# Turning attention probabilities with VectorE block transposes and DMAs instead of TensorE, and repeating the feed-forward q and k by DMA

## What is computed

```python
xn = layernorm(x)
# branch 1: 16 heads of 64, causal
q, k, v = split(xn @ W_qkv);  q, k = rotary(q), rotary(k)
weights = softmax(where(mask, q @ k.T / 8, -1e9))
y = (weights @ v) @ W_out
# branch 2: 16 heads of 8, not causal, then a layer of 8 experts, top 2
q, k, v = xn @ Wq + bq, xn @ Wk + bk, xn @ Wv + bv
ctx = softmax(q @ k.T / sqrt(8)) @ v
x2 = xn + layernorm(ctx @ Wo + bo) * g1 + be1
moe = top2 experts of x2, weighted by the gate's softmax
out = x + y + x2 + layernorm(moe) * g2 + be2
```

## Time and profile before

| what | value |
|---|---|
| median of 3 runs (lowest, highest) | 1271.35 us (1267.77, 1273.54) |
| span of the profiled execution | 1270.3 us |
| TensorE busy in it | 1159.3 us (91%) |
| VectorE busy | 928.0 us (73%) |
| ScalarE busy | 892.0 us (70%) |
| GpSimd busy | 811.5 us (64%) |
| mean granted TensorE clock | 0.978 |

### The profile page before, as it was taken

One profiled execution on the slowest core, in us unless ns is written; L12 is line 12 of the kernel. 1 busy time (PEld: TensorE's weight loads), 2 busy tenths in 40 slices (PEclk: granted clock), 3 DMA queues, 4 the chain that ended last, 5 costly groups with the idle time before them and its releaser, 6 DMA issues.

```text
span 1270.3 us, 25325 instructions
## 1 busy us (share of the span) xinstructions
PE 1159.3 (91%) x9387; PEld 741.3 (58%) x9387; DVE 928.0 (73%) x2336; ACT 892.0 (70%) x1841; POOL 811.5 (64%) x730
## 2 busy tenths in 40 slices
PE   4779999999999999999999999999999999899986
PEld 3355565655666565655656556665656556575655
DVE  7666487885878857896687848787687866778546
ACT  3567867487766868578775887668776796748860
POOL 3655774577855767568864778467675587645760
PEclk8799999999999999999999999999999999999998
DMA  4000100011000110001100011001000011000000
GB/s 144 34 34 18 43 35 17 26 39 38 34 18 26 51 43 26 18 26 59 39 13 35 26 43 42 18 26 51 34 29 24 25 35 51 18 17 34 34 18 9
DMA packets 34110, 42.87 MB, mean 34 GB/s; under 512 B 5694, under 2 KB 17216, under 8 KB 33988
## 3 DMA queue, kind: packets, MB, share of 16 engines
q1 hardware_dynamic: 30516, 38.31, 8.2%
q10 hardware_dynamic: 3472, 2.95, 0.8%
HBM read 5.60 MB, written 2.10 MB: 6 GB/s over the span
## 4 chain that ended last, share of the span: by engine, by line
PE 59%; DVE 17%; ACT 14%; issue 4%; POOL 4%; DMA 1%; SPq 0%; ACTq 0%; DVEq 0%; POOLq 0%
PE work L1319 7%; PE work L1233 7%; PE work L1334 6%; PE work L1346 6%; PE work L1235 6%; PE work L1234 6%; PE work L1396 5%; DVE fnmax L1071 5%; ACT fpt L884 5%; PE work L1362 4%; ACT pn L926 4%; DVE work L1193 3%; PE work L1371 3%; PE work L1386 3%; ACT pt L938 2%
## 5 line engine op out<-in xcount | busy, mean ns | idle before, releaser
L926 ACT ACTIVATE pn<-work,nmax 128x512 f32<-128x512 f32 (+3 forms) x512 | 265.3, 534 | 119.9 <-DVE nmax L1193 119.4
L785 POOL TENSOR_TENSOR raw<-raw,cos_t 128x512 f32<-128x512 f32 x128 | 163.8, 1280 | 284.9 <-DMA swapped<-raw 269.7
L1071 DVE TENSOR_REDUCE fnmax<-work 128x2 f32<-128x1024 f32 x256 | 302.0, 1219 | 47.0 <-PE work L1371 45.8
L1193 DVE CUSTOM_DVE_ANT_0 work<-work,causal 128x512 f32<-128x512 f32 (+3 forms) x512 | 236.1, 520 | 95.5 <-PE work L1319 94.7
L884 ACT ACTIVATE fpt<-work 128x1024 f32<-128x1024 f32 x256 | 252.4, 1029 | 52.7 <-PE work L1386 51.4
L1334 PE MATMUL work<-consts,pn 128*128 128x128 f32 x1280 | 172.6, 277 | 7.0 <-DVE fnmax L1071 4.0
L789 POOL TENSOR_TENSOR raw<-raw,swapped 128x512 f32<-128x512 f32 x128 | 163.7, 1279 | 10.0
L1334 PEld LDWEIGHTS work<-consts,pn 128*128 128x128 f32 x1280 | 141.1, 141 | 42.7 <-DVE fnmax L1071 13.0
L800 POOL TENSOR_TENSOR qk_l<-raw,qk_h 128x512 fp32r<-128x512 f32 x128 | 163.3, 1282 | 2.8
L786 POOL TENSOR_TENSOR swapped<-swapped,sin_t 128x512 f32<-128x512 f32 x128 | 163.7, 1279 | 0.0
L938 ACT COPY pt<-work 128x1024 f32<-128x1024 f32 x128 | 130.4, 1019 | 42.6 <-PE work L1334 42.1
(11 more groups left out here) (161 smaller groups left out, 2140.1 us busy)
## 6 DMA issues: line engine op xcount, KB each, us to landing
swapped<-raw SPq DMA_DIRECT2D x256, 128.0 KB, 2.0
x_in<-in_L_attn_x_dram SPq DMA_DIRECT2D x8, 256.0 KB, 3.4
out_dram<-x_in SPq DMA_DIRECT2D x7, 256.0 KB, 2.2
fpt<-in_L_attn_W_qkv_dram ACTq DMA_DIRECT2D x3, 512.0 KB, 5.9
pt<-in_L_ffn_We_dram ACTq DMA_DIRECT2D x1, 512.0 KB, 7.2
wout<-in_L_attn_W_out_dram ACTq DMA_DIRECT2D x1, 512.0 KB, 8.4
out_dram<-x_in SPq DMA_DIRECT2D x2, 128.0 KB, 1.8
pt<-in_rope_dram ACTq DMA_DIRECT2D x1, 192.0 KB, 6.5
```

The lines of the kernel that those rows point to most:

```text
L785: nc.gpsimd.tensor_tensor(raw[:, n % 3], raw[:, n % 3], cos_t[:], ALU.mult)
L926: ins = nc.scalar.activation(pn[:, h, PN_AT[j]:PN_AT[j] + n], bank_of(("sc", b, c, unit), h)[:, at:at + n], ACT.Exp, scale=-1.0, bias=nmax ...
L1071: nc.vector.tensor_reduce(fnmax[:, j, 2 * r:2 * r + 2, 0:1], bank_of(("fsm", b, g, j), 2 * r, 2).rearrange("p (f n) -> p f n", f=2), AX.X, ...
L1193: ins = nc.vector.tensor_tensor_reduce(out=scores, in0=scores, in1=causal[:, S - n:S], scale=-1.0 / math.sqrt(DH), scalar=3.0e38, op0=ALU.add,
```

## The change

The steps `tp`, `tq`, `tpe` and `tqe` go. `exp` writes its columns so that column 4r+q of a tile lies in block q at place r. A new DVE step `tr` turns each 32x32 block of `pn` in place (three instructions a head pair, over 1024, 1024 and 512 elements a partition). A new SP step `shuf` issues four DMAs, each from the 32 partitions of one block row of `pn` to all 128 partitions of `pt`; 327,680 bytes each. `pn` now has two buffers and `pt` one. `pv` takes its first key tile in two products (384 and 128 columns instead of 512), reads `pt` in runs of 32 elements, and its columns run over the query tiles backwards; `rT` and `ao` follow that order. `l_rows` goes: `fan` writes `l_wide`, `rb` overwrites it, and `fan` waits for the `div` before it.

`fqk` is done once a batch instead of once a group, with the plain 128 columns of Wq and Wk; `fqkh` and `fqkl` too. A new SP step `fdup` issues three DMAs a group that copy the high and low rows of q and k into the strips (131,072 bytes each). The table of start times is replaced by a table of places in each engine's list, and the banks are given anew for every batch.

```diff
-WIDE = {"tt": 2, "fqk": 2, "fsm": 4, "fst": 4, "moe": 2, "v": 2, "sc": 2, "tp": 2}
+WIDE = {"tt": 2, "fqk": 2, "fsm": 4, "fst": 4, "moe": 2, "v": 2, "sc": 2}
-        pn = sb("pn", [P, 2, PT_N])
-        pt = sb("pt", [P, 2, 2, PT_N])
-        l_rows = sb("l_rows", [P, S])
+        pn = sb("pn", [P, 2, QUADS, 2, PT_N, STRIP])
+        pt = sb("pt", [P, QUADS, 2, PT_N, STRIP])
-        fqk = sb("fqk", [P, 2, 2, S], F32R)
+        fqn = sb("fqn", [P, 4, S], F32R)
+        fqs = sb("fqs", [P, 2, 2, S], F32R)
+        fqm = sb("fqm", [P, S], F32R)
...
 SP
+                elif kind == "shuf":
+                    c = x_[2]
+                    wait(sp, after("tr", b, c, 2))
+                    wait(sp, after("pv", *ring(1, b, c, NC)))
+                    for a in range(QUADS):
+                        sp.dma_start(pt[:, a].rearrange("p h n r -> p (h n r)"),
+                                     pn[a * STRIP:(a + 1) * STRIP, c % 2].rearrange("p c h n r -> p c (h n r)")).then_inc(shuf_done[c % 2], 16)
+                elif kind == "fdup":
+                    g = x_[2]
+                    wait(sp, after("fqkl", b))
+                    wait(sp, after("fst", *ring(2, b, g, G), T - 1))
+                    for c, pair in ((1, slice(0, 4, 2)), (2, slice(1, 3)), (3, slice(0, 4, 3))):
+                        sp.dma_start(fqs[c:P:4, g % 2].bitcast(F32), fqn[g * STRIP:(g + 1) * STRIP, pair].bitcast(F32)) .then_inc(fdup_done[g % 2], 16)
...
 ACT, fqkh
-                    wait(act, after("fqk", b, g))
-                    wait(act, after("fst", *ring(2, b, g, G), T - 1))
-                    for k, low in enumerate((q_low, k_low)):
-                        ins = nc.scalar.activation(fqk[:, g % 2, k], bank_of(("fqk", b, g), k), ACT.Identity, scale=low,
-                                                   bias=qk_less[:, k, g:g + 1])
+                    wait(act, after("fqk", b))
+                    wait(act, *(landed("fdup", b - 1, g) for g in range(G)))
+                    for k in range(2):
+                        ins = nc.scalar.activation(fqn[:, 2 * k], bank_of(("fqk", b), k), ACT.Identity, bias=qk_bias[:, k:k + 1])
 ACT, exp
                     if unit == 0:
-                        wait(act, after("tp", *ring(1, b, c, NC), 1))
-                        wait(act, after("tq", *ring(1, b, c, NC)))
+                        wait(act, landed("shuf", *ring(2, b, c, NC)))
                     for j, at in SM_UNITS[unit]:
-                        ins = nc.scalar.activation(pn[:, h, PN_AT[j]:PN_AT[j] + n], bank_of(("sc", b, c, unit), h)[:, at:at + n],
+                        ins = nc.scalar.activation(pn[:, c % 2, :, h, tiles].rearrange("p c i r -> p i r c"),
+                                                   bank_of(("sc", b, c, unit), h)[:, at:at + n].rearrange("p (i r c) -> p i r c", r=STRIP, c=QUADS),
...
 DVE
-                elif kind == "tqe":
...
+                elif kind == "tr":
+                    c, unit = x_[2:]
+                    wait(dve, after("exp", b, c, unit, 0), after("exp", b, c, unit, 1))
+                    blocks = pn[:, c % 2, :, :, UNIT_TILES[unit]].rearrange("p c h n r -> p c h (n r)")
+                    nc.vector.transpose(blocks, blocks).then_inc(done["tr"], 1)
...
 PE, fqk
-                        ins = split3(bank_of(x_, k), wh, wl, xt_h[:, b % 2], xt_l[:, b % 2])
+                        ins = split3(bank_of(x_, k), wqk_h[:, k], wqk_l[:, k], xt_h[:, b % 2], xt_l[:, b % 2])
-                elif kind in ("tp", "tq"):
...
-                                        ins = nc.tensor.transpose(dst[:, at + (j - i) * P:at + (j - i + 1) * P],
-                                                                  pn[:, h, from_:from_ + P], ident)
 PE, pv
-                    wait(pe, after("tpe", b, c, 0), after("tpe", b, c, 1))
-                    wait(pe, after("tqe", b, c))
+                    wait(pe, landed("shuf", b, c))
-                    for i in range(T):
+                    for i, js in ((0, (3, 2, 1)), (0, (0,)), (1, (3, 2, 1)), (2, (3, 2)), (3, (3,))):
+                        first, at = TILES_OF[js[0]] + i, (T - 1 - js[0]) * P
...
+                            moving = pt[:, :, h, first:first + 4 * len(js) - 3:4] if len(js) > 1 else pt[:, :, h, first:first + 1]
+                            ins = nc.tensor.matmul(psum[a:a + STRIP, at:at + len(js) * P], v[:, i, 2 * c + h, a % DH:a % DH + STRIP],
+                                                   moving.rearrange("p a j r -> p j a r"),
 PE, fsm of j = 0
-                        wait(pe, after("fqkl", b, g))
+                        wait(pe, landed("fdup", b, g))
```

More of the change, by code:

```diff
@@ L464, in later @@
-def later(kind, b, n):
-    own = {0: FIRST, B - 1: LAST}.get(b, {}).get(kind)
-    return own[n] if own else SHIFT.get(kind, {}).get(b, 0)
-ENGINE = {
-    "PE": ("tt", "tb", "xT", "fv", "fqk", "fsm", "fmT", "fst", "fpv", "fT", "cT", "wo", "x2T", "gate", "moe", "proj", "v", "sc", "tp",
-           "tq", "pv", "rT", "ao"),
-    "ACT": ("tab", "wh", "smh", "weh", "xh", "fvc", "fqkh", "fexp", "fo", "ch", "x2h", "gexp", "raw", "vc", "exp", "tpe", "fan", "rb"),
-    "DVE": ("res_last", "out_last", "turn", "str", "strl", "qkb", "wl", "sml", "bia", "wel", "ln", "xn", "xl", "fqkl", "fmax", "fsub", "fdiv", "cl", "ln1", "nm1", "x2l", "gsub", "pick", "moew", "ln2", "nm2",
-            "max", "tqe", "inv", "div", "yadd"),
-    "POOL": ("rs0", "rs1", "rs2", "rope", "hi", "lo", "x2", "res", "out"),
-    "SP": ("swap", "store", "load"),
-}
+    "xT": ["5", "0", "0", "0", "0", "0", "0", "0"],
@@ new lines @@
+    "tt": ["0"],
+    "proj": [
+        "1104165657725023", "0270460761746020", "6244566467706065", "0754562767706041", "0757566757760020",
+        "5054567227765000", "6774562627712010", "3574561667766072",
+    ],
+    "tb": ["7"],
+    "fqk": ["5", "5", "5", "5", "5", "5", "5", "5"],
+    "fv": ["5", "5", "6", "4", "6", "5", "7", "5"],
+    "fsm": [
+        "4040402040402022", "4310402042402020", "4110401042402021", "4100402042402021", "4410402042402020",
+        "4100402042402021", "4110042042402023", "4410402042402022",
+    ],
@@ new lines @@
+ENGINE = {
+    "PE": ("tt", "tb", "xT", "fv", "fqk", "fsm", "fmT", "fst", "fpv", "fT", "cT", "wo", "x2T", "gate", "moe", "proj", "v", "sc", "pv", "rT", "ao"),
+    "ACT": ("tab", "wh", "smh", "weh", "xh", "fvc", "fqkh", "fexp", "fo", "ch", "x2h", "gexp", "raw", "vc", "exp", "fan", "rb"),
+    "DVE": ("res_last", "out_last", "turn", "str", "strl", "qkb", "wl", "sml", "bia", "wel", "ln", "xn", "xl", "fqkl", "fmax", "fsub", "fdiv", "cl", "ln1", "nm1", "x2l", "gsub", "pick", "moew", "ln2", "nm2",
+            "max", "tr", "inv", "div", "yadd"),
+    "POOL": ("rs0", "rs1", "rs2", "rope", "hi", "lo", "x2", "res", "out"),
+    "SP": ("swap", "shuf", "fdup", "store", "load"),
+}
@@ L501 @@
         KEYS[kind] = [()]
-TIME = {(kind, b) + key: PERIOD * b + at + later(kind, b, n) for kind in START
-        for b in range(1 if kind in ONCE else B) for n, (key, at) in enumerate(zip(KEYS[kind], START[kind]))}
-for b in range(B - XB, B):
-    del TIME["load", b]
-LAST_ON_DVE = {"res": ("yadd", B - 1, 1), "out": ("nm2", B - 1)}
-for kind, x in LAST_ON_DVE.items():
-    del TIME[kind, B - 1]
-    TIME[kind + "_last", B - 1] = TIME[x] + 1e-3
-ORDER = {engine: sorted((x for x in TIME if x[0] in kinds), key=TIME.get) for engine, kinds in ENGINE.items()}
+BATCHES = {kind: [0] if kind in ONCE else [B - 1] if kind in LAST_ON_DVE_STEPS else range(len(rows)) for kind, rows in PLACE.items()}
+AT = {(kind, b) + key: at for kind, rows in PLACE.items() for b, row in zip(BATCHES[kind], rows) for key, at in zip(KEYS[kind], row)}
+LAST_ON_DVE = ("res", "out")
+ORDER = {engine: sorted((x for x in AT if x[0] in kinds), key=AT.get) for engine, kinds in ENGINE.items()}
 COUNT = {}
@@ L542, in place @@
             continue
-        homes = LAST_PSUM.get(x[0], PSUM[x[0]]) if x[1] == B - 1 else PSUM[x[0]]
-        i = first[x] = homes[[y for y in KEYS[x[0]] if x[0] != "fpv" or y[1] == 0].index(x[2:])]
+        homes = [y for y in KEYS[x[0]] if x[0] != "fpv" or y[1] == 0]
+        i = first[x] = int(PSUM[x[0]][x[1]][homes.index(x[2:])])
         before[x] = [y for y in holder[i:i + WIDE.get(x[0], 1)] if y is not None]
@@ L857, in _ @@
                     wait(act, after("proj", b - 2, NC - 1, 1))
-                    wait(act, after("fqk", b - 2, G - 1))
+                    wait(act, after("fqk", b - 2))
                     wait(act, after("v", b - 2, T - 1))
@@ L920, in _ @@
                     if unit == 0:
-                        wait(act, after("tp", *ring(1, b, c, NC), 1))
-                        wait(act, after("tq", *ring(1, b, c, NC)))
+                        wait(act, landed("shuf", *ring(2, b, c, NC)))
+                        if b == 0 and c < 2:
+                            for kind_ in LOADED:
+                                wait(act, after(kind_, 0))
                         wait(act, after("inv", *ring(2, b, c, NC)))
@@ L929, in _ @@
```

(17 more changed lines are left out.)

1073 lines of the change are left out of this document (626 added, 447 removed), and 277 rows, old and new, of tables (FIRST, LAST, LAST_PSUM, PLACE).

## The result

The changed kernel takes 1427.8 us (median of 4 runs, 1420.5 to 1430.5), the kernel before 1272.4 us: a ratio of 1.121 (95% interval 1.117 to 1.126). It is 12% slower, where 1162 us and 8.6% faster had been forecast; the range ended at 1245. The page, for the earlier trace rows and part of the earlier trace rows: span, busy time, slices, SP's queue, the chain that ended last, issues.

A forecast was written before the change was run, and what follows sets the result against it. TensorE was taken to bound the kernel before, VectorE the changed one. Start 58, middle 955 / 0.929 = 1028, end 75 and 1 outside the span sum to 1162 us, 8.6% faster; range 1100 to 1245.

The forecast's parts named there:

- the transfers: Four DMAs a pair from pn to pt, 1.31 MB: taken at 5.2 us, other end 15 us, expected hidden.
- rival 2: Slow transfers: at 15 us a landing, the loop of one pt is 17.3 us a pair, in all 1208 us; chance 0.10.
- GpSimd's slack of 5 us a pair covers it.: Swaps queued on SP behind shuf can come up to 5.2 us late; GpSimd's spare time was to absorb that.
- rival 5: The new order or its waits, SP's queue above all, eat the gain: 1271 us; chance 0.05.
- The strided `exp`: ScalarE's exp writes 2560 bytes apart: no extra cost taken; each added step an element 136 us, one (863 us) still hidden.
- The share of the middle: Between 60 and 1200 us of the kernel before: VectorE to be busy 92.9%, so 955 us of work takes 1028.
- TensorE's clock: No drop expected at 87% busy; even a mean of 0.93 stretches 978 us to about 1045, just level with VectorE.
- The transposes: Three block transposes a pair on VectorE: 3.13 us a pair at one element a step, 200 us taken.
- VectorE's total: VectorE's busy time after removed copies and added transposes: 1049 us, the highest of all engines.
- ScalarE without the strides: ScalarE's busy time after removed copies and fqk operations, with strided writes costing nothing: 727 us.
- TensorE's removed products for q and k: 48 of 64 product triples on the strips go at 0.82 us each: 39 us off TensorE.
- TensorE's total: TensorE's busy time: 1159 less 150 for transposes and 39 for products, plus 8 for the product with v: 978 us.

The follow-up runs named there:

- e2: Changed kernel with each of a pair's four transfers carrying only the first 64 elements (256 bytes instead of 2560) of each row; 1266.3 us, ratio 0.996.
- e5: Changed kernel with each transfer reading one 2560-byte piece from each of 128 partitions instead of four from each of 32; output wrong; 1279.1 us, ratio 1.006.
- e12: Whole change with transfers in order 0, 2, 1, 3, new lists for all engines including TensorE, and new banks; 1318.7 us.
- e3: Changed kernel with both exp writing in runs and transfers cut to 256 bytes a row; output wrong; 1225.6 us, ratio 0.962.
- e10: Kernel before, with exp writing each tile's columns 128 bytes apart instead of next to each other; output wrong; 1341.3 us, ratio 1.055.
- e7: Changed kernel with score products reading keys in order 4r+q, so exp writes runs of 32 elements; whole computation; 1421.8 us.
- e14: Changed kernel with exp in runs and short transfers, plus new lists for all engines and new banks; output wrong; 1223.6 us.
- e6: Changed kernel with a pair's four transfers issued in block order 0, 2, 1, 3 instead of 0, 1, 2, 3; whole computation; 1376.3 us.
- e9: Changed kernel with transfers in order 0, 2, 1, 3 and new lists for SyncE, ScalarE, VectorE and GpSimd; TensorE's list and banks kept; 1322.3 us.
- e4: Kernel before with only the q and k part of the change (made once a batch, repeated by three DMAs a group), old lists; 1269.7 us, ratio 0.997.
- e1: Changed kernel with exp writing its elements in runs instead of 2560 bytes apart; output wrong; 1414.7 us.

## Why the prediction was wrong

**The step that failed first: the transfers.** "I take 5.2 (same queue, rows of like size)". The rows were not alike in what mattered: the swaps read from 64 partitions, these from 32. The path took 9.07 us on the chain and 9.5 in the median. The other end of the bound was 15 us, so the size was inside it; rival 2 priced it at 1208 us by the loop of the one `pt`. That mechanism doesn't explain the loss. SP's waits for the product before, in the changed kernel and in e2 (us, times, longest):

```profile
SPq L1089 <- PE work L1699: 123.1, 32, 12.1
...
SPq L1089 <- PE work L1700: 134.0, 30, 16.3
```

Half of the pairs wait, but as many and as long in e2, which has the same one buffer and takes 1266 us. What a second `pt` would give in any of these kernels was not run. How the 4 us more turned into 149 us (e5) or 161 (e2) is read from the trace and not split by a run: SP's list has swaps behind each transfer, TensorE's list has `pv` in front of other work, and then TensorE's clock falls. In e5 TensorE is busy 1055.6 us at a mean clock of 0.906, in the changed kernel 1111.3 us at 0.862 for the same work: busy time times clock is 956 to 958 us in both, so the 56 us more are the clock's.

**"GpSimd's slack of 5 us a pair covers it."** It didn't. GpSimd is busy the same 812 us, but its wait rose by 158 us; with cheap transfers it is 260. Slack on average did not keep single swaps from coming late, up to 16.8 us. This was rival 5's mechanism, which had a chance of 0.05 and 1271 us. By e12 the wait in itself is not the price.

**The strided `exp`.** "I take none; one added step (863 us) would stay hidden too". One added step it was, 1.73 instead of 0.83 ns an element, and ScalarE stood at 828 us; but it did not stay hidden. It cost 13 us behind the slow transfers, 41 without them (e2 to e3), and 69 in the kernel before (e10). The nearest row, reads on VectorE with a wide step, was another engine and another direction. The Trainium skill's text on cachelines ("SBUF — State Buffer", the port swizzle's section) was right in direction: consecutive accesses to different 16-byte lines cost. Here ScalarE's writes cost double, and e7 shows a price for TensorE's reads 16 bytes apart. No run has a step inside one line, so that the line is the reason is the page's word.

**The share of the middle.** The forecast gave VectorE 92.9% of the middle. With the two prices at or below the forecast's (e3, e14) it holds 85%. The middle of e14 is 1090 us where 1028 had been forecast, which is the last 62 us (1224 against 1162); VectorE even had 25 us less to do there (930 against 955). New lists didn't move it. TensorE's clock had been dismissed: "At 87% I expect no drop. Even at a mean of 0.93, TensorE's 978 us would stretch to about 1045". At 0.907 TensorE is busy 1043 us, beside VectorE's 1027: two engines level, each at 84 to 85% of the span. Whether the clock, the waits of the two for each other, or the one `pt` keeps them there is open: no run held the clock up or added a buffer.

**The lists.** "The new order or its waits eat the gain" was a rival, not a term. New lists for the durations found took 54 us off (e6 to e9) and nothing off e3 (e14). They can't be charged with a loss of their own: they are of use only for given durations.

**What held.** The transposes (199 us, forecast 200), VectorE's total (1033, forecast 1049), the bytes, ScalarE without the strides (741, forecast 727), and TensorE's removed products for q and k: 1122.7 in e4 is 37 us less, forecast 39. TensorE's total did not hold (978 forecast; 1111 at a clock of 0.862, 1043 at 0.907).

Added up from the forecast: 1162, plus 64 to e3, plus 41 for `exp` to e2, plus 161 for the transfers, gives 1428. The parts hang on the order: with `exp` taken off first it is 13 us, and the transfers 189 (e1 to e3).

## What to carry to other kernels

Price a DMA between tiles by how many partitions each transfer reads at a time, and not by its bytes alone: the same rows took twice as long from 32 partitions as from 128. A price on an engine with room need not be hidden when every unit of work passes through it in order (69 us for `exp` on ScalarE at 73%); what it costs is read from a run with that price alone. And before a relief on the bound engine is called worthless, lay out the lists anew for it: here it gave 0.3% alone, new lists 0.5% alone, both together 3.0%.

## What the runs showed of the hardware that was not expected

- A transfer of 320 KB in 2560-byte rows landed in 5.7 us from 32 partitions and in 2.9 us from 128; two queues that each read from 32 partitions gave 5.7 and 6.1, interleaving blocks 0, 2, 1, 3 in one queue 5.0. From the first issue to the last landing of four such transfers the medians were 9.5 us (changed kernel), 8.7 (two queues), 8.6 (interleaved) and 5.0 (128 partitions).
- SP's issue of such a transfer took 0.6 us for the first two of four and 1.8 to 2.0 for the other two (medians); in e5 and e2, where transfers landed in 2.9 and 1.9 us, all four took some 0.6 or less.
- ScalarE's `exp` of fp32 cost 1.73 ns an element with writes 2560 bytes apart, 1.77 at 128 bytes, 0.83 next to each other.
- TensorE's score products of 512 columns took 721 instead of 522 ns when the keys lay 16 bytes apart.
- TensorE's mean granted clock was 0.978 in the kernel before (91% busy), 0.906 in e5 (83%), and 0.862 in the changed kernel (78%) and in e7 (83%). The share alone doesn't tell the clock, and a low clock itself makes the busy time longer.
